# Expert blocks with 64-row remainders, a third weight buffer, and pair weights found by matmul in the route

## The chip, the cores and the metric

The kernel runs on one core of one Trainium2 chip. The metric is device time in microseconds; three runs of the kernel before gave a median of 1706.33 us (1705.12 to 1709.56). All times in the profile are microseconds from the start of its span unless marked ns.

## What is computed

The input x has 4 sequences of 512 tokens with 256 features (2048 tokens, 16 tiles of 128), and a context of 4 x 64 tokens. Four layers follow each other, each with an attention and a feed-forward part. Three of the feed-forward parts are mixtures of experts, and only these are touched:

```
logits = x @ router                      # 8 experts (7 in layer 1)
top2, weights of the two                 # every token has TOP = 2 pairs
for each token t and its experts e:
    y[t] += w[t, e] * (silu(xn[t] @ Wg[e]) * (xn[t] @ Wu[e])) @ Wd[e]
```

Layer 0 (stage `e0`) has 8 experts with a hidden width of 704, layer 3 (`e3`) has 8 with 512, layer 1 (`e1`) has 7 with 256 and a shared expert beside them. Everything is float32. Which expert gets how many of the 4096 pairs is known only at run time.

## The kernel before, in words

The stages run one after the other: attention `a0`, experts `e0`, attention `a1`, layer 1's attention `l1`, experts `e1`, lookup and FP4 feed-forward `f2`, attention `a3`, experts `e3`. `experts` (L1790 on) calls `normalise`, `route` and, for layers 0 and 3, `blocks`; for layer 1 `kept_blocks`, which is not changed.

**route** (L1951 on) ranks the pairs by expert. TensorE counts and ranks them into the bank `small`; VectorE turns the counts into the first block of each expert, each pair's slot, the owner (expert) of each block, and one-hot tables `place_hot` (place in the block) and `at_hot` (which block). Two tables of `numbers` are filled by GpSimd from `at_hot` (L2083), two by VectorE. 32 matmuls (L2035) then find, for each slot, the number of its pair; VectorE makes of it the row of the token, `token`, and `pair`, the address of the pair's weight. ScalarE writes the two weights of every token into `weight_of`, and SyncE copies that table to DRAM (`w_pairs`, L2062) and waits for it, on the same queue on which late weights were sent before. TensorE fills its waits with products that nobody reads (`stay_busy`, L360): 20, 44 and 16 of 512 columns. GpSimd last gathers the rows of the first two blocks (L2095). The stage ends when all engines are through.

Layers 0 and 3 use the simple layout: every expert's pairs are rounded up to whole blocks of 128 rows, and the number of blocks is its worst case,

```
ROUTED = (TOP * B * S + NE * (P - 1)) // P        # 39
```

Layer 1 already uses `Layout(7, 32)`: 28 full blocks, and 6 mixed ones of four quarters with an expert each, which its route lays out by a longer chain of small steps (L2173 to L2204).

**blocks** (L2297 on) works through the 39 blocks in order, in a hardware loop of two blocks. The queues for block n are:

- SyncE: `load_gate_up` (L1868) reads the owner into a register and loads gate and up weights of the expert, two transfers (704 KB each in layer 0, 512 KB in layer 3), into one of two buffers `wgu`, as soon as the up product two blocks earlier is done. The down weights of all experts lie in SBUF.
- GpSimd: gathers the rows of block n (`fetch`, L2353) two blocks ahead, sends the results of block n - 4 by an adding scatter into `y_sum` (`send`, L2367), and gathers the 128 weights of a block (`fetch_weight`, L2359). A send waits until the send before has landed.
- TensorE: gate product of block n, the expert's number into a register, turning the rows of block n + 1, up product of n, down product of n - 1. The gate and up products have 128 x 128 pieces of the weights as the stationary side and 128 turned rows moving, 2 per chunk of 128 hidden columns (L2394); the down product has the hidden rows stationary and 256 columns moving (L2418).
- ScalarE: silu (L2454). VectorE: copies the turned rows (L2466), multiplies gate and up (L2473), and weighs the result while it copies it (L2481); in layer 0 it also quantises a chunk of the FP4 weights every second block (`rounds.round`), 18 in all.

In the end SyncE waits for the sends; in layer 3 it then copies `y_sum` to the output.

## Time and profile before

| | us |
|---|---|
| median of 3 runs | 1706.33 |
| profiled execution, its own time | 1702.23 |
| its span | 1700.0 |
| TensorE matmul busy | 1486.8 (87%) |
| TensorE weight loads busy | 1125.1 (66%) |
| VectorE, ScalarE, GpSimd busy | 941.7, 536.2, 509.6 |
| mean granted TensorE clock | 0.947 |
| stage e0: route from 146.6, blocks from 176.0, tail to about 491 | |
| stage e3: route from 1435.3, blocks from 1462.0, end 1700 | |

PE is TensorE, PEld its weight loads, DVE VectorE, ACT ScalarE, POOL GpSimd, SP SyncE; PEq and SPq are the sequencers of TensorE and SyncE. The profiled execution is one of the kernel's executions, 4.1 us below the median. PEclk is the granted clock of TensorE as a share of 2.4 GHz. A float32 matmul shows as two records. Matmul ends are modelled, so starts are the safer marks.

### The profile page before, as it was taken

To read this page: it belongs to the slowest core of one execution; us is meant where nothing else is said; L and a number is where in the kernel's file an instruction comes from. 1 tells how busy PE (TensorE), PEld (TensorE's weight loads), DVE (VectorE), ACT (ScalarE), POOL (GpSimd) and SP (SyncE) were. 2 spreads that over 40 slices of the span, in tenths; PEclk is the share of its full clock that TensorE was granted. 3 is DMA by queue.
4 is the path that set the end of the run, shared out by engine and by line. 5 is a ranking of instruction groups with operands and counts; after the bars stand their busy time and mean duration, and the time that the engine had idled before them with its cause. 6 is when DMAs were issued, how large, how long until landed. Compare 5 with 4: busy or idle time off the path is not lost. (4 is left out here: it accounts for less than half of the span.)

```text
span 1700.0 us, 33505 instructions
## 1 busy us (share of the span) xinstructions
PE 1486.8 (87%) x11960; PEld 1125.1 (66%) x11961; DVE 941.7 (55%) x2396; ACT 536.2 (32%) x1143; POOL 509.6 (30%) x549
## 2 busy tenths in 40 slices
PE   4887899999979987799987999668888888899995
PEld 3664799999967863355554555346666665699995
DVE  4556244444438977766645633579877566422221
ACT  2331111111137754455542256233322333011010
POOL 0102344444410002111112223345342110466663
PEclk9999999999988998899998999889989999999998
DMA  4109677777720005434304122210000005588885
GB/s 142 49 2 299 215 221 220 221 219 222 218 79 1 2 1 153 131 99 115 90 21 151 64 88 82 68 41 19 1 1 1 1 2 179 180 243 240 233 237 148
DMA packets 127860, 199.85 MB, mean 118 GB/s; under 512 B 20224, under 2 KB 77312, under 8 KB 127552
## 3 DMA queue, kind: packets, MB, share of 16 engines
q1 hardware_dynamic: 107104, 169.15, 30.7%
q0 software_dynamic: 20640, 29.16, 8.3%
q8 instruction: 72, 1.18, 0.3%
q14 instruction: 44, 0.36, 0.1%
HBM read 165.71 MB, written 34.64 MB: 118 GB/s over the span
## 5 line engine op out<-in xcount | busy, mean ns | idle before, releaser
L1576 DVE TENSOR_REDUCE l1a_nm<-l1a_sc 128x1 f32<-128x512 f32 (+3 forms) x256 | 107.1, 482 | 53.7 <-PE l1a_sc L1712 53.7
L2454 ACT ACTIVATE e0b_sg<-e0b_gp 128x640 f32<-128x640 f32 x78 | 33.5, 481 | 266.2 <-PE e0b_gp L2394 266.2
L2367 POOL DMA_INDIRECT y_sum<-e0b_yb,e_token x39 | 63.1, 1619 | 140.6 <-DVE e0b_yb L2481 137.6
L2454 ACT ACTIVATE e3b_sg<-e3b_gp 128x512 f32<-128x512 f32 x39 | 23.3, 597 | 190.0 <-PE e3b_gp L2394 190.0
L2367 POOL DMA_INDIRECT y_sum<-e3b_yb,e_token x39 | 62.7, 1607 | 61.5 <-DVE e3b_yb L2481 58.6
L1710 PE MATMUL l1a_sc<-l_stack_k,l_stack_q 128*128 128x512 bf16 (+3 forms) x256 | 59.1, 309 | 16.7 <-PEq L1354 14.9
L1710 PEld LDWEIGHTS l1a_sc<-l_stack_k,l_stack_q 128*128 128x128 bf16 x256 | 25.3, 99 | 60.8 <-issue 26.8
L2473 DVE TENSOR_TENSOR e0b_hT<-e0b_up,e0b_sg 128x640 f32<-128x640 f32 x39 | 32.1, 824 | 57.8 <-PE e0b_up L2394 57.8
L1471 POOL TENSOR_TENSOR xn<-xn 128x512 f32<-128x512 f32 x8 | 10.1, 1265 | 178.2 <-DVE xn L1439 178.2
L2394 PEld LDWEIGHTS e0b_gp<-e0b_xT,e0k_wgu 128*128 128x128 f32 x480 | 58.4, 197 | 1.9 <-DVE e0b_xT L2466 0.9
L1246 DVE TENSOR_REDUCE a_nm<-a_sc 128x8 f32<-128x512 f32 x64 | 39.7, 683 | 35.8 <-PE a_sc L1096 35.8
L2394 PE MATMUL e0b_gp<-e0b_xT,e0k_wgu 128*128 128x128 f32 x480 | 58.7, 280 | 0.5 <-DVE e0b_xT L2466 0.5
L2473 DVE TENSOR_TENSOR e3b_hT<-e3b_up,e3b_sg 128x512 f32<-128x512 f32 x39 | 27.0, 691 | 57.6 <-PE e3b_up L2394 57.6
L1738 PE MATMUL l1a_st<-l_stack_q,l_stack_k 128*128 128x512 bf16 (+3 forms) x256 | 56.6, 302 | 0.0
L2575 PE MATMUL e1b_gu<-e_kgu,e1b_xT 128*128 x112 | 54.6, 611 | 1.7 <-DVE e1b_xT L2670 1.7
L2394 PEld LDWEIGHTS e0b_gp<-e0b_xT,e0b_wgu 128*128 128x128 f32 x456 | 53.8, 192 | 2.5 <-issue 1.5
L2394 PE MATMUL e0b_gp<-e0b_xT,e0b_wgu 128*128 128x128 f32 x456 | 54.1, 275 | 1.4 <-DVE e0b_hT L2473 1.4
L1190 POOL CAST a_nmp<-a_nm 128x32 bf16<-128x32 f32 x16 | 8.8, 553 | 154.2 <-DVE a_nm L1246 154.2
L3256 PE MATMUL f_yp<-f2w_down,f_hT 128*128 128x256 f32 x192 | 49.6, 413 | 4.6 <-DVE x L3110 4.0
L2541 POOL DMA_INDIRECT e_xb<-x_rows,e_token x32 | 30.2, 945 | 77.8 <-PE e1b_xp L2560 67.3
L2481 DVE TENSOR_SCALAR e0b_yb<-e0b_yp,e0k_weight 128x256 f32<-128x256 f32 x39 | 18.9, 484 | 62.4 <-PE e0b_yp L2418 62.4
L2466 DVE COPY e3b_xT<-e3b_xp 128x256 f32<-128x256 f32 x39 | 16.5, 424 | 58.4 <-PE e3b_xp L2388 58.4
(645 smaller groups left out, 4099.7 us busy)
## 6 DMA issues: line engine op xcount, KB each, us to landing
e3k_wgu<-in_L_ffn_W SPq DMA_DIRECT2D x40, 512.0 KB, 4.9
e3b_wgu<-in_L_ffn_W SPq DMA_DIRECT2D x38, 512.0 KB
e0k_wgu<-in_L_ffn_gate_proj SPq DMA_DIRECT2D x20, 704.0 KB, 4.3
e0k_wgu<-in_L_ffn_up_proj SPq DMA_DIRECT2D x20, 704.0 KB, 5.5
e0b_wgu<-in_L_ffn_gate_proj SPq DMA_DIRECT2D x19, 704.0 KB, 4.3
e0b_wgu<-in_L_ffn_up_proj SPq DMA_DIRECT2D x19, 704.0 KB, 5.6
x_rows<-xn SPq DMA_DIRECT2D x3, 2048.0 KB, 8.4
l_parts<-l1p_split SPq DMA_DIRECT2D x16, 384.0 KB, 3.1
```

Of the source, the lines that this page charges most:

```text
L1246: nc.vector.tensor_reduce(nm[:, :, r, :], bank[r][:].rearrange("p t (h l) -> p t h l", l=L), AX_X, ALU.max, negate=True).then_inc(max_done, 1)
L1576: nc.vector.tensor_reduce(nm[:, g % 2, q, i:i + 1], sc[q], AX_X, ALU.max, negate=True).then_inc(max_done, 1)
L1710: nc.tensor.matmul(sc[q], of_head(1, n)[:, q * P:(q + 1) * P], of_head(0, n)[:, 0:(q + 1) * P], start=True, stop=False)
L1738: nc.tensor.matmul(to(k), of_head(0, n)[:, k * P:(k + 1) * P], of_head(1, n)[:, k * P:], start=False, stop=False)
L2367: pool.indirect_dma_start(y_sum, bass.IndirectOffsetOnAxis(ap=token[:, n:n + 1], axis=0), yb[n % 2][:], None, compute_op=ALU.add).then_inc ...
L2394: last = nc.tensor.matmul(dst[:, f, :], wgu[j][:, k, at + f * P:at + (f + 1) * P], xT[j][:, k, :], start=(k == 0), stop=(k == KC - 1))
L2454: last = nc.scalar.activation(sg[rows, chunks, :], gp[rows, chunks, :], ACT.Silu)
L2473: last = nc.vector.tensor_tensor(hT[j][rows, chunks, :], from_up, sg[rows, chunks, :], ALU.mult)
L2481: nc.vector.tensor_scalar(yb[j][:], yp[:], plan.weight[:, bass.ds(n, 1)], None, ALU.mult).then_inc(y_copied, 1)
L2541: pool.indirect_dma_start(xb[n % 2][:], None, x_rows, bass.IndirectOffsetOnAxis(ap=token[:, order[n]:order[n] + 1], axis=0))\
L2575: last = nc.tensor.matmul(gu[n % 2][:], xT[n % 2][:, k, :], wgu[:, bass.ds(e, 1), k, :].rearrange("p a f -> p (a f)"), start=(k == 0), sto ...
L3256: last = nc.tensor.matmul(yp[:], hT[:, f, :], dT[:, f, :], start=(f == 0), stop=(f == FC - 1))
```

## The change

- The layout of layers 0 and 3 becomes `HALVES = Layout(8, 64)`: 32 full blocks and 4 mixed ones of two halves of 64 rows, each with an expert of its own, 36 blocks and 40 units of weights. The mixed blocks stand at positions 4, 13, 22 and 31 of the order. Layer 1 keeps its layout; its tables lose 5 columns.
- Three buffers `wgu` instead of two; a load waits for the up product of the block that used the buffer last.
- In a mixed block the turned rows are the stationary side, 64 columns per half, and up to 512 columns of the half's own weights move; the hidden rows are then turned by TensorE (`turn_hidden`), copied by ScalarE, and the down product takes its second half's weights from `mixed_d`, which ScalarE has copied beforehand.
- A mixed block is sent twice, each time with the other half's rows directed to spare rows.
- The weight of each slot's pair is split into three bf16 parts, multiplied into `at_hot` (three products on GpSimd, three on VectorE), found by 32 more matmuls in the route and summed by VectorE. The DRAM table, its write and the 39 gathers per layer are gone. The last `stay_busy` of the route has 10 products instead of 16.
- The loops over blocks are written out instead of run in hardware loops, and TensorE reads the expert's number right ahead of the down product.

```diff
-ROUTED = (TOP * B * S + NE * (P - 1)) // P
+HALVES = Layout(NE, P // 2)
 QUARTERS = Layout(NE - 1, P // 4)
+ROUTED = HALVES.blocks
...
@@ SummedBlocks
-            self.weight_of = ...; self.pair = ...
+            self.HELD = 3
+            self.send = st.enter_context(nc.sbuf_tensor(f"{tag}k_send", [P, HALVES.owners], U32))
@@ route, TensorE, behind the matmuls that find the tokens
                     if plan is not None:
-                        stay_busy(idle[:], 16)
+                        pe.wait_ge(weighted, 3 * TOP)
+                        for t in range(T):
+                            for k in range(TOP):
+                                last = nc.tensor.matmul(found_weight, place_hot[k][:, t, :], weight_hot[k][:, t, :, :],
+                                                        start=(t + k == 0), stop=(t == T - 1 and k == TOP - 1))
+                        last.then_inc(weight_made, 1)
+                        stay_busy(idle[:], 10)
@@ route, SyncE
-                        sp.wait_ge(tabled, 1)
-                        sp.wait_ge(weighed, 3)
-                        sp.dma_start(w_pairs.rearrange("(p n) a -> p (n a)", p=P), plan.weight_of[:]).then_inc(tabled, 16)
-                        sp.wait_ge(tabled, 17)
@@ route, GpSimd
+                        (weight_part[0..2]: five operations of 32 columns, once the weights are there)
                     pool.wait_ge(step, 30)
                     (numbers[0], numbers[1])
+                    if plan is not None:
+                        pool.wait_ge(parted, 5)
+                        for i in range(3):
+                            nc.gpsimd.tensor_tensor(weight_hot[1][:, :, i, :], at_hot[1][:], bcast(weight_part[i][:, :, 1], 2, NB), ALU.mult)\
+                                .then_inc(weighted, 1)
                     (gathers of the first two blocks' rows)
@@ route, VectorE: layout of all layers by full and odd parts (the old simple branch goes), and before the token
+                        for i in range(3):
+                            nc.vector.tensor_tensor(weight_hot[0][:, :, i, :], at_hot[0][:], bcast(weight_part[i][:, :, 0], 2, NB), ALU.mult)\
+                                .then_inc(weighted, 1)
...
+                        dve.wait_ge(weight_made, 1)
+                        nc.vector.tensor_reduce(plan.weight[:, 0:NB], found_weight.rearrange("p i b -> p b i"), AX_X, ALU.add)
@@ blocks, SyncE
+                    for k in range(1, len(block_of)):
+                        if k >= plan.HELD:
+                            sp.wait_ge(up_made, block_of[k - plan.HELD] + 1)
+                        plan.load_gate_up(sp, owner, owner_of[k], k % plan.HELD)
@@ blocks, GpSimd
-                    def fetch_weight(n): ...
                     def send(n):
                         pool.wait_ge(y_copied, n + 1)
+                        for i, (block_n, at, done, value) in enumerate(sent):
+                            if block_n == n:
+                                if i:
+                                    pool.wait_ge(*sent[i - 1][2:])
+                                pool.indirect_dma_start(y_sum, bass.IndirectOffsetOnAxis(ap=plan.send[:, at:at + 1], axis=0), yb[n % 2][:],
+                                                        None, compute_op=ALU.add).then_inc(done, 16)
@@ blocks, TensorE
+                        if is_mixed(n):
+                            for lo in range(0, chunks * P, BANK):
+                                hi = min(lo + BANK, chunks * P)
+                                for k in range(KC):
+                                    for u, unit in enumerate(units_of[n]):
+                                        rows = slice(u * HALF, (u + 1) * HALF)
+                                        last = nc.tensor.matmul(flat(dst)[rows, lo:hi], xT[n % 2][:, k, rows],
+                                                                wgu[unit % plan.HELD][:, k, at + lo:at + hi], start=(k == 0), stop=(k == KC - 1))
...
+                    for n in range(NB):
+                        gate(n)
+                        if n + 1 < NB:
+                            turn_rows(n + 1)
+                        if n and is_mixed(n - 1):
+                            turn_hidden(n - 1)
+                        up_product(n)
+                        ... down(n - 1)
@@ blocks, VectorE
+                        if rounds is not None and n % 2:
+                            rounds.round(dve, n // 2)
+                    weigh_out(NB - 1)
```

## Rows read from the trace of the kernel before

**Rows 1.** Windows of the block stages: span, busy by engine (count), granted clock, DMA share, GB/s.

```profile
176.00:187.40 11.40, 9.46 (x52) 7.89 (x53) 2.27 (x6) 2.14 (x3) 3.77 (x4) 0.71 0.46 151
187.40:484.00 296.60, 295.93 (x2214) 283.55 (x2214) 131.81 (x331) 32.61 (x76) 133.36 (x110) 1.00 0.71 212
1469.00:1683.00 214.00, 212.35 (x1602) 202.33 (x1602) 60.83 (x114) 22.69 (x38) 130.78 (x110) 1.00 0.78 226
```

**Rows 2.** Timeline of TensorE, a block of layer 0: start us, us, instructions.

```profile
434.57 2.84 PE L2394 MATMUL e0b_gp<-e0b_xT,e0b_wgu 128*128 128x128 f32 x24
...
439.70 1.03 PE L2418 MATMUL e0b_yp<-inner,e0b_hT 128*128 x4
...
442.29 2.84 PE L2394 MATMUL e0b_gp<-e0b_xT,e0k_wgu 128*128 128x128 f32 x24
```

**Rows 3.** Chain that ended last: a block of layer 3, and the tail.

```profile
1657.64 1.78 PE e3b_gp L2394 x16
1659.42 0.22 PE e3b_xp L2388 x2
1659.64 1.79 PE e3b_up L2394 x16
1661.43 1.73 PE e3b_yp L2418 x8
...
1679.53 0.49 DVE e3b_yb L2481
...
1680.87 3.68 DMA y_sum<-e3b_yb,e_token
...
1685.10 1.79 POOLq L2326
```

**Rows 4.** Timeline of TensorE in layer 1: a full block's gate and up, a mixed block's.

```profile
977.10 1.88 PE L2575 MATMUL e1b_gu<-e_kgu,e1b_xT 128*128 x4
...
980.22 1.92 PE L2572 MATMUL e1b_gu<-e1b_mixed_gu,e1b_xT 128*32 128x512 f32 x16
```

**Rows 5.** DMA issues: KB each, median us to landing.

```profile
e3k_wgu<-in_L_ffn_W SPq DMA_DIRECT2D x40, 512.0 KB, 4.9
e3k_xb<-x_rows,e_token POOLq DMA_INDIRECT x39, 4.7
```

**Rows 6.** Timeline of VectorE in the routes of layer 1 and layer 3.

```profile
935.63 0.16 DVE L2173 TENSOR_SCALAR e1r_held_i<-e1r_small 128x8 uint32<-128x8 f32 x1
...
938.99 0.85 DVE L2214 TENSOR_TENSOR e1r_past<-consts,e1r_begins 128x676 f32<-128x676 f32 x1
...
1441.36 0.17 DVE L2156 COPY e3r_cnt<-e3r_small 128x8 f32<-128x8 f32 x1 [1.11 <-PE e3r_small L2022]
...
1443.54 0.44 DVE L2211 TENSOR_TENSOR e3r_past<-consts,e3r_first 128x273 f32<-128x273 f32 x1
```

**Rows 7.** Line 2083, GpSimd: duration ns min/median/max, first and last start.

```profile
L2083 POOL TENSOR_TENSOR e0r_numbers<-e0r_at_hot,consts x2: 3150/3216/3281, 158.7 to 161.8; 128x624 bf16<-128x624 f32 x2
L2083 POOL TENSOR_TENSOR e1r_numbers<-e1r_at_hot,consts x2: 1235/2258/3282, 943.8 to 944.9; 128x624 bf16<-128x624 f32 x2
L2083 POOL TENSOR_TENSOR e3r_numbers<-e3r_at_hot,consts x2: 3221/3252/3283, 1447.3 to 1450.4; 128x624 bf16<-128x624 f32 x2
```

**Rows 8.** Timeline of TensorE: end of layer 3's route and start of its blocks.

```profile
1455.70 5.30 PE L360 MATMUL e3r_idle<-ones_h,ident_h 128*128 128x512 bf16 x16
...
1462.07 1.02 PE L360 MATMUL e3b_gp<-ones_h,ident_h 128*128 128x512 bf16 x4 [1.07 <-PEq L2005]
```

**Rows 9.** Timeline: end of layer 0's route and start of its blocks.

```profile
166.33 3.32 SPq L2062 DMA_DIRECT2D w_pairs<-e0k_weight_of  x1
...
176.05 1.86 PE L360 MATMUL e0b_gp<-ones_h,ident_h 128*128 128x512 bf16 x4 [3.98 <-PEq L2005]
```

**Rows 10.** DMA queue of instructions in layer 0's and in layer 1's blocks: packets, MB, share.

```profile
q8 instruction: 3, 0.05, 0.1%
...
q8 instruction: 5, 0.08, 0.3%
```

More of the change, by code:

```diff
@@ L195, in build @@
     rows_out = [pool_sem(f"rows_out{j}") for j in range(2)]
-    weight_in = [pool_sem(f"weight_in{j}") for j in range(2)]
     rows_summed = [pool_sem(f"rows_summed{j}") for j in range(2)]
@@ L2416, in down, with turn_hidden @@
+                    def turn_hidden(n):
                         pe.wait_ge(h_done, n + 1)
                         for f in range(FC):
-                            last = nc.tensor.matmul(yp[:], hT[j][:, f, :],
+                            width = min(P, F - f * P)
+                            last = nc.tensor.transpose(hp[0:width, f, :], h[:, f * P:f * P + width], ident)
+                        last.then_inc(h_turned, 1)
+                    def down(n):
+                        if n:
+                            pe.wait_ge(y_copied, n)
+                        own = lay.owner_at(order[n])
+                        e = pe.value_load(owner[0:1, own[0]:own[0] + 1], min_val=0, max_val=plan.E - 1)
+                        first = slice(0, P // len(own))
+                        if is_mixed(n):
+                            pe.wait_ge(mixed_ready, (mixed_at.index(n) + 1) * FC)
+                            pe.wait_ge(h_copied, mixed_at.index(n) + 1)
+                        else:
+                            pe.wait_ge(h_done, n + 1)
+                        for f in range(FC):
+                            last = nc.tensor.matmul(yp[first, :], hT[n % 2][:, f, first],
@@ L2445, in _ @@
-                    down(NB - 1, 0, expert(NB - 1))
+                    stay_busy(flat(gp)[:, 0:S], 4)
+                    turn_rows(0)
+                    for n in range(NB):
+                        gate(n)
[4 more added lines that the diff above has]
+                        up_product(n)
+                        if n == 0:
+                            if LEFT:
+                                pe.wait_ge(padded, 2)
+                            pe.wait_ge(plan.kept, plan.all_kept)
+                        else:
+                            down(n - 1)
```

444 lines of the change are left out of this document (209 added, 235 removed).

## The prediction

> **What bounds the kernel now.** I read the windows by stage first, because only the two stages that the change rebuilds matter: the expert blocks of layer 0 and of layer 3. In both, TensorE works 295.9 of 296.6 us and 212.4 of 214.0 us at a granted clock of 1.00, VectorE is busy less than half, and the DMA engines 0.71 and 0.78 [rows 1]. So these stages last as long as TensorE's instructions, and taking a block out takes its whole TensorE time out. The timeline then gives a block of layer 0: from one gate product to the next 442.29 - 434.57 = 7.72 us, of which the down product is 2.59 [rows 2]. The chain that ended last gives a block of layer 3 with no gap in it: gate 1.78, turning the rows 0.22, up 1.79, down 1.73, together 5.52 us; and it shows the tail, where two sends into y_sum stand in a row, each waiting for the one before to land [rows 3].
>
> **Blocks.** The old bound on blocks is 39, all of 128 rows; the new layout has 32 full and 4 mixed, 36. That removes 3 blocks per layer: 3 x 7.72 + 3 x 5.52 = 39.7 us off, all on the path.
>
> A mixed block multiplies the turned rows (64 wide, two units) as the stationary side with up to 512 weight columns moving, instead of 128 x 128 pieces. The rows for that are the mixed blocks of layer 1: four units side by side make 16 matmul records in 1.92 us, where a full block makes 4 records over the same columns in 1.88 [rows 4]. So outputs on separate partitions run beside each other, and what counts is the moving columns, which are the same 768 + 640 (layer 0) or 512 + 512 (layer 3) as in a full block. I take gate, up and down as unchanged, with the 0.04 us of rows 4 once. What a mixed block adds on TensorE is turning the hidden rows: 6 or 4 transposes at 0.22 / 2 = 0.11 us [rows 3], with the 0.04 some 0.7 and 0.5 us. Four each: 4.8 us. ScalarE's copy out of PSUM and its copies of the second expert's down weights lie beside the up product; VectorE does the same elements. If units did not share TensorE at all, see the first rival. The Trainium skill, "TensorE: Matmul & The Clock Gate", section "Measured speedup vs the span model", gives 2.38 times for three column tiles, not three times. By that rule, applied to two halves (an estimate: 1.6 instead of 2), the sum would be about 13 us more, 1692; the trace's four tiles disagree, since 1.92 against 1.88 is nearly full overlap.
>
> The register load of the expert's number moves on TensorE's queue from behind the gate product to behind the up product. It stands behind 1.79 us of queued matmuls instead of 1.78 [rows 3], so I cost it at nothing; without that cover every block would pay it.
>
> **Loads.** There are 40 unit loads instead of 39, over 36 blocks. A load is issued when an up product ends and lands 4.9 us after its issue in layer 3 [rows 5]; it is needed one block and one down product later, 5.52 + 1.73 = 7.25 us. The third buffer keeps this slack where two units fall into one block, so nothing waits, though DMA work per microsecond grows by 40/36 = 1.11, towards a share of 0.78 x 1.11 = 0.87 at most, less the gathers of weights that go. The row gathers (4.7 us to landing, [rows 5]) now stand on POOL's queue behind a send that may wait for another send, but two blocks ahead of use.
>
> **Route.** Its steps are serial on VectorE. (a) Layout by full and odd parts: in layer 1, which already does this, count to ownership takes 938.99 - 935.63 = 3.36 us, in layer 3 now 1443.54 - 1441.36 = 2.18: +1.18. (b) The ownership test and its sum grow from 273 to 600 elements: 0.44 now, 0.85 for 676, so about 0.76: twice +0.32. (c) Wrapping the owner, two more small steps, +0.2. Sum +2.0 us [rows 6].
> (d) POOL. The two products that fill `numbers` took 3.2 us each for 624 elements beside a busy VectorE, but 1.24 once when layer 1's VectorE was not in its long products [rows 7]. The change adds three more of that kind on POOL (576 elements), and TensorE's new weight products wait for them. Per product 1.14 (free) to 3.0 us (contended). In layer 3: start 1447.3 + 2.0, two numbers 6.0, then the three, of which the first is contended and the others mostly free, 5.6 (bounds 3.4 and 9.0): 1460.9. POOL's own first two row gathers queue behind this, where they used to start from the token alone.
> (e) TensorE: 32 products of 108 columns, then 10 idle-time products. The 16 of before took 5.30 us, a mix of both clocks [rows 8]; from 0.21 to 0.43 per 512 columns the 32 cost 1.4 to 2.9 and the ten 2.1 to 4.3. I take 2.4 + 3.0, since TensorE stands still before found and again before weights. End 1466.3, plus the 1.07 of changing blocks [rows 8]: 1467.3 against 1462.07 now. **+5.2 us** (bounds +1 and +10). What goes, VectorE's shorter token chain and the table write, ended earlier here and gives nothing.
> In layer 0 the same steps start at 158.7 and end at 158.7 + 2.0 + 6.0 + 5.6 + 2.4 + 3.0 + 1.07 = 178.8. There the old end is later, 176.05, with TensorE still for 3.98 us before: the table write of w_pairs is issued at 166.33, behind the late weights on the same queue [rows 9]. That wait goes; +2.7 us remain. But the stillness also cost clock: the first 11.4 us of blocks had a granted clock of 0.71 [rows 1], 3.3 us of lost time. With idle-time products up to 1 us before, as in layer 3, I take 3.0 of it back: **-0.3 us** (bounds -4 and +8).
> Layer 1 changes only by fewer columns beside a busy TensorE: 0.
>
> **Sends.** Removed: 39 weight gathers per layer, which lie on POOL and DMA, off the path: 0. Added: a second send per mixed block, chained. From rows 3 a chained send takes 4.5 (copy 1680.02 to landing 1684.55) to 5.1 us (to the next issue, 1685.10), say 4.8. In layer 0 the delay 2 x 4.8 - 7.72 = 1.9 is gone one block later. In layer 3 it is 2 x 4.8 - 5.52 = 4.1, recovered by 0.7 per block. The last mixed block is number 31 of 0 to 35, so 4.1 - 2 x 0.7 = **+2.7 us** reach the tail (1.4 to 3.8).
>
> **Sum.** -39.7 + 4.8 + 5.2 - 0.3 + 2.7 = -27.3 us on the profiled execution's 1702.2 (span 1700.0 and 2.2 around it): 1674.9. The median of the runs shown is 4.1 higher, so 1679.
>
> **Rivals.**
> *A, the halves take turns (0.05).* A pair of 64-wide products would run one after the other. Place: the mixed blocks. Price: gate, up and down a second time, 4 x 7.5 + 4 x 5.3 = 51 us: 1679 + 51 = 1730, slower than before. It decides from the point where 27 of the 51, a little over half of the second unit's time, is exposed. Against it: [rows 4], though those are 32 wide.
> *A2, they share only in part (0.03).* The same place with a quarter of the second unit's time exposed: 51 / 4 = 13 us, 1692. For and against as A. The skill's 2.38 for three tiles would lie near this.
> *B, code loading (0.04).* The loops become straight code. Now 3 fetches fall into 297 us of layer 0's blocks; layer 1's unrolled blocks make 5 in 110 us with light DMA [rows 10]. Unrolled, layer 0 and 3 would need about 30, beside DMA engines at 0.8. A fetch with no lead at all would cost up to a row gather's 4.7 us [rows 5]; at 2 us each it is 60 us: 1739. For it only that no row has both conditions; against it that layer 1's blocks have no such gap. The Trainium skill, "Runtime: NRT & Kernel Launch", section "Instruction fetch mechanics", says sequential code is fetched ahead and taken branches are what stall; by that this rival falls.
> *C, a queue runs late at mixed blocks (0.15).* The load slack in layer 3, 7.25 - 4.9 less the time to issue two transfers, is under 2.4 us, and the row gather behind two chained sends has 2 x 5.52 us less the sends' 9.6. If each of the 8 mixed blocks costs 1 to 2 us of waiting: 1687 to 1695.
> *D, the route at its upper bounds (0.1):* +5 and +8 more: 1692. At its lower bounds (0.06): 1671.
> Forecast as summed: 0.57.
>
> **Numbers.** Predicted 1679. The range runs from both routes at their low bounds to C or D: 1669 to 1693, leaving A, B and joint mishaps out. 0.3% is 5 us, about what a measurement of this kernel can tell. Faster by more: 0.91 (forecast, A2, C, D). Within it: 0.02, a half-exposed A or B. Slower: 0.07 (rest of A and B).
>
> **What would show it.** 36 gate groups per layer; full blocks at 7.72 and 5.52 us; mixed ones at 8.4 and 6.0, the pair's records ending together. Records in turn would show A, TensorE idle with no releaser B, TensorE waiting for a wgu or xb transfer after blocks 4, 13, 22, 31 C. In the routes, POOL's five products ahead of the gathers, block stage starts near 179 and 5 us later than now. Weight matmuls that don't wait for POOL would prove (d) wrong, and a tail of the old length the sends' term.

## The result, and the profile after

| us | before | after |
|---|---|---|
| median (range) of 5 runs each | 1706.33 (1702.2 to 1709.6) | 1719.04 (1715.3 to 1724.1) |
| profiled execution, its span | 1702.23, 1700.0 | 1723.26, 1721.4 |
| mean granted TensorE clock | 0.947 | 0.934 |

The ratio of the times is 1.0092, 95% interval [1.0073, 1.0112]: the change makes the kernel slower by 0.9%, where 1679 us, 1.6% faster, was predicted. The two profiled executions lie 21 us apart, because one is at the low end of its runs and the other near the high end; the stages below are compared within one execution each.

Windows of the block stages after, same columns as [rows 1]: the start of layer 0's blocks, then both stages, then 9 us around one break.

```profile
182.20:190.80 8.60, 6.64 (x53) 5.84 (x53) 2.27 (x6) 3.17 (x6) 1.89 (x2) 1.00 0.78 292
190.80:480.00 289.20, 281.34 (x2054) 252.19 (x2055) 121.91 (x314) 39.56 (x95) 93.76 (x71) 0.98 0.71 220
1481.50:1697.00 215.50, 204.03 (x1452) 179.08 (x1452) 55.24 (x104) 27.80 (x53) 90.58 (x69) 0.97 0.78 228
399.00:402.00 3.00, 2.44 (x12) 2.44 (x13) 2.79 (x10) 0.00 (x0) 2.20 (x2) 0.50 0.15 11
402.00:405.00 3.00, 3.00 (x14) 2.91 (x14) 1.33 (x4) 0.00 (x0) 1.56 (x2) 0.50 0.37 76
405.00:408.00 3.00, 3.00 (x17) 2.65 (x17) 1.13 (x3) 0.00 (x0) 1.66 (x2) 0.94 0.54 102
```

TensorE is no longer busy throughout: 7.9 us are missing in layer 0 and 11.5 in layer 3 (0.7 and 1.6 in [rows 1]), though 3 blocks are gone from each. Around each break the granted clock is 0.50, for 3.4 us at the first and the third and for 6.8 us at the second and the fourth. The breaks, in TensorE's timeline:

```profile
322.81 0.44 PE L2387 MATMUL e0b_xp<-consts,e0k_xb 128*128 128x128 f32 x2 [2.61 <-DMA e0k_xb<-x_rows,e_token]
...
399.56 0.69 PE L2387 MATMUL e0b_xp<-consts,e0k_xb 128*128 128x128 f32 x2 [3.94 <-DMA e0k_xb<-x_rows,e_token]
...
1578.50 0.44 PE L2387 MATMUL e3b_xp<-consts,e3k_xb 128*128 128x128 f32 x2 [3.23 <-DMA e3k_xb<-x_rows,e_token]
...
1636.45 0.69 PE L2387 MATMUL e3b_xp<-consts,e3k_xb 128*128 128x128 f32 x2 [4.68 <-DMA e3k_xb<-x_rows,e_token]
```

Each time a row gather is late. From gate product to gate product these blocks take 12.18, 14.63, 10.62 and 12.56 us in place of 7.72 and 5.52, so with the slow clock behind them the four breaks cost 4.5 + 6.9 + 5.1 + 7.0 = 23.5 us. What was late stands in GpSimd's waits (us in total, times, longest), where the kernel before waited for `y_sum` once in each layer:

```profile
POOL y_sum L2371 <- DMA y_sum<-e0b_yb,e0k_send: 110.2, 24, 6.6
...
POOL y_sum L2371 <- DMA y_sum<-e3b_yb,e3k_send: 56.6, 21, 4.7
```

GpSimd's timeline from the first mixed block of layer 0 on shows how it comes about:

```profile
231.73 1.59 POOL L2371 DMA_INDIRECT y_sum<-e0b_yb,e0k_send  x1 [5.18 <-DVE e0b_yb L2527]
237.72 1.57 POOL L2371 DMA_INDIRECT y_sum<-e0b_yb,e0k_send  x1 [4.40 <-DMA y_sum<-e0b_yb,e0k_send]
239.59 1.01 POOL L2360 DMA_INDIRECT e0k_xb<-x_rows,e_token  x1 [0.30 <-issue]
244.61 1.58 POOL L2371 DMA_INDIRECT y_sum<-e0b_yb,e0k_send  x1 [4.00 <-DMA y_sum<-e0b_yb,e0k_send]
246.49 1.02 POOL L2360 DMA_INDIRECT e0k_xb<-x_rows,e_token  x1 [0.30 <-issue]
253.01 1.58 POOL L2371 DMA_INDIRECT y_sum<-e0b_yb,e0k_send  x1 [5.50 <-DMA y_sum<-e0b_yb,e0k_send]
```

The second send (237.72) goes out when the first has landed, and the sends that follow it wait for the one before: the queue runs at the pace of its own landings, 6.0, 6.9, 8.4 us, and a row gather stands behind each send. SyncE's timeline has the loads beside them:

```profile
237.00 0.38 SPq L1872 DMA_DIRECT2D e0b_wgu<-in_L_ffn_gate_proj  x1
...
244.71 0.38 SPq L1872 DMA_DIRECT2D e0b_wgu<-in_L_ffn_gate_proj  x1
```

In the kernel before, a send went out 2.7 us after a load (435.64 after 432.97) and landed 4.3 us after its issue (median), 7.0 after the load's. Now it goes out together with the load (237.72 and 237.00) and the next one can go only 6.9 us later, at 244.61, again together with a load (244.71). The delay keeps itself up, one send per load, and each mixed block adds one link.

The DMA packets tell what is late, the rows themselves or only the report of their landing. In the profile's DMA view, packets of GpSimd's transfers are `software_dynamic`, those of SyncE's loads `hardware_dynamic`. After the issue at 237.72, first up to 242.0 and then from 242.0 to 243.5 (packets, MB, share):

```profile
q1 hardware_dynamic: 460, 1.25, 90.6%
...
q0 software_dynamic: 178, 0.25, 76.2%
q1 hardware_dynamic: 84, 0.19, 32.6%
```

The 128 rows of the send are among the 178: the first moves 4.5 us after the issue (242.24), beside the last packets of the load, and the last has moved by 243.50, 1.1 us before the next send goes out (244.61). So it is the rows that are late. Over all sends of layer 0's blocks the median time from the issue to the first row's packet is 2.4 us in the kernel before and 4.5 us in the changed one.

Layer 3 is less regular: there the steps between sends behind the first mixed block run from 4.5 to 7.6 us, and the seven from 1512.66 to 1550.36 are 5.4 us in the mean, where a block takes 5.52. At the end the late sends hang behind the last product. The chain that ended last, to be read against the tail in [rows 3]:

```profile
1698.13 3.78 DMA y_sum<-e3b_yb,e3k_send
...
1702.64 3.85 DMA y_sum<-e3b_yb,e3k_send
```

The copy to the output goes out at 1711.05, 23.1 us after the last gate product's start (1687.97); before it was 15.1.

### The profile page after: what moved, and what is told of

Its sections match the earlier page's. It is cut to its first block and busy times, and to the rows that moved or that the text cites. A ratio compares the mean times of both kernels' runs of the same rounds, so it can differ in the third digit from the quotient of the medians.

```text
span 1721.4 us, 31704 instructions
## 1 busy us (share of the span) xinstructions
PE 1467.2 (85%) x11688; PEld 1079.2 (63%) x11720; DVE 942.6 (55%) x2399; ACT 550.3 (32%) x1182; POOL 439.3 (26%) x483
## 5 line engine op out<-in xcount | busy, mean ns | idle before, releaser
L2371 POOL DMA_INDIRECT y_sum<-e0b_yb,e0k_send x40 | 63.0, 1574 | 180.8 <-DMA y_sum<-e0b_yb,e0k_send 110.2
L2480 ACT ACTIVATE e0b_sg<-e0b_gp 128x640 f32<-128x640 f32 x64 | 27.5, 482 | 221.6 <-PE e0b_gp L2402 221.6
L2371 POOL DMA_INDIRECT y_sum<-e3b_yb,e3k_send x40 | 62.9, 1572 | 120.1 <-DVE e3b_yb L2527 63.5
L1713 PE MATMUL l1a_sc<-causal_h,ident_h 128*128 128x128 bf16 x256 | 46.7, 222 | 20.7 <-PEq L1355 16.2
L2520 DVE TENSOR_TENSOR e0b_hT<-e0b_up,e0b_sg 128x640 f32<-128x640 f32 x32 | 26.4, 825 | 55.5 <-PE e0b_up L2402 53.8
L1739 PE MATMUL l1a_st<-l_stack_q,l_stack_k 128*128 128x512 bf16 (+2 forms) x254 | 56.1, 301 | 0.0
L2527 DVE TENSOR_SCALAR e3b_yb<-e3b_yp,e3k_weight 128x256 f32<-128x256 f32 x36 | 17.4, 484 | 65.1 <-DMA y_sum<-e3b_yb,e3k_send 37.2
L1711 PE MATMUL l1a_sc<-l_stack_k,l_stack_q 128*128 128x256 bf16 (+3 forms) x226 | 50.0, 295 | 2.1 <-DVE l1a_nm L1577 1.8
L2402 PE MATMUL e0b_up<-e0b_xT,e0b_wgu 128*128 128x128 f32 x400 | 51.6, 288 | 0.0
L2402 PEld LDWEIGHTS e0b_up<-e0b_xT,e0b_wgu 128*128 128x128 f32 x400 | 49.9, 205 | 0.0
```

Of the source, the lines that this page charges most:

```text
L1711: nc.tensor.matmul(sc[q], of_head(1, n)[:, q * P:(q + 1) * P], of_head(0, n)[:, 0:(q + 1) * P], start=True, stop=False)
L1713: last = nc.tensor.matmul(sc[q][:, q * P:(q + 1) * P], ident_h[:], causal_h[:], start=False, stop=True)
L1739: nc.tensor.matmul(to(k), of_head(0, n)[:, k * P:(k + 1) * P], of_head(1, n)[:, k * P:], start=False, stop=False)
L2371: pool.indirect_dma_start(y_sum, bass.IndirectOffsetOnAxis(ap=plan.send[:, at:at + 1], axis=0), yb[n % 2][:], None, compute_op=ALU.add).th ...
L2402: last = nc.tensor.matmul(dst[:, f, :], wgu[units_of[n][0] % plan.HELD][:, k, at + f * P:at + (f + 1) * P], xT[n % 2][:, k, :], start=(k = ...
L2480: last = nc.scalar.activation(sg[rows, chunks, :], gp[rows, chunks, :], ACT.Silu)
```

## Experiments

Times are medians, "ratio" is to the kernel before in runs on the same chip, with its 95% interval. Each diff is against the changed kernel unless it says otherwise.

**No mixed blocks.** `HALVES = Layout(NE, P)`: 39 whole blocks, the rest of the change kept.

> The changed kernel with no mixed block: both experts layers again run 39 blocks of 128 rows of one expert each (7.72 and 5.52 us), one send per block; three weight buffers, the blocks written out one by one and the weights found by TensorE stay. Chain theory (the second send of a mixed block puts the queue of sends one load behind, and each send then waits for the one before): with one send per block POOL waits for y_sum under 10 us in all, sends land in 3.6 to 5.0 us, no gap of TensorE for xb inside the blocks; only the longer routes (+3.5 and +5.9) and the first gate product on a faster clock (-2.8) are left: 1706 + 5 to 8, so 1710 to 1715 us. Three-buffers theory (loads bunched by the third buffer delay the row gathers): the breaks of 2.6 to 4.7 us stay, and with two more blocks each the time is 1735 or more. Code loading: gaps on several engines at once stand in the blocks, 1725 or more.

1716.73 us, ratio 1.0074 [1.0049, 1.0099]. GpSimd waits for `y_sum` not at all in e0 and 9.2 us in e3, sends land in 4.4 and 4.3 us, no break, full blocks 7.72 and 5.52. So neither the third buffer nor the straight code breaks anything. Without a single mixed block the change still costs 11 to 13 us, where at most 9 were expected; the run with the route alone, below, comes back to this.

**One send per mixed block.** The second half is not sent; its rows are missing from the result.

```diff
-                for at in lay.owner_at(order[n]):
+                for at in lay.owner_at(order[n])[:1]:
```

> The changed kernel, with the send of the second half of every mixed block left out (so these rows of the result are missing); products, loads and gathers as they are. Chain theory: POOL waits for y_sum under 10 us in each layer, landing back at 3.6 to 5.0 us, the four breaks (4.5, 6.9, 5.1 and 7.0 us) are gone and the tails shorter by 1 to 3 us each: 1719 - 23.5 - 4 = 1691 us (1688 to 1696). Three-buffers theory: sends have little to do with it, the row gathers are late as before, 1712 or more.

1690.04 us, 0.9904 [0.9873, 0.9936]: the eight sends left out are worth 29 us. No break. In e0 the waits for `y_sum` are gone; in e3 the expectation of under 10 us was wrong, they are still there, only never long enough to stop TensorE:

```profile
POOL y_sum L2371 <- DMA y_sum<-e3b_yb,e3k_send: 49.3, 15, 5.8
```

**No loads.** Gate and up weights are loaded for three units only.

```diff
-                    for k in range(1, len(block_of)):
+                    for k in range(1, plan.HELD):
...
-                            pe.wait_ge(gu_in[unit % plan.HELD], 32 * (unit // plan.HELD + 1))
+                            pe.wait_ge(gu_in[unit % plan.HELD], 32)
```

> The changed kernel with the weights of gate and up loaded for the first three units only (later blocks multiply by stale ones, the result is wrong in value but the work of the engines is the same); both sends of a mixed block stay. Theory that a send beside a weight load lands when the load ends: without loads a send lands in 4.3 us or less throughout, the second sends are caught up within one block, no breaks: 1719 - 23.5 - 4, near 1691 us, perhaps less by the waits for a load. Theory that the added send is slow of itself, or that POOL's own issue work takes the time: the landing stays at 6 to 8 us and the breaks stay, 1710 or more.

1684.85 us, 0.9876 [0.9849, 0.9903], with both sends of every mixed block. The landing of a send, in the answer for its tile (min/median/max), of e0:

```profile
DMA to landing us min/median/max: 3.7/3.8/4.3
```

From issue to the first row's packet it is now 2.1 us in the median, with the work of VectorE and GpSimd the same. GpSimd still waits for `y_sum`, 17.7 us in e0 and 42.4 in e3, but never over 3.2 us: in e3 the steps behind a second send are 4.6 us of a block of 5.52, so the queue catches up by 1 us per block, and there is no break. So the second send alone stops nothing; it takes loads beside it.

**Half the rows in the first send**: partitions 0 to 63.

```diff
-pool.indirect_dma_start(y_sum, bass.IndirectOffsetOnAxis(ap=plan.send[:, at:at + 1], axis=0), yb[n % 2][:],
+rows = slice(0, lay.unit if at >= lay.full and (at - lay.full) % lay.per == 0 else P)
+pool.indirect_dma_start(y_sum, bass.IndirectOffsetOnAxis(ap=plan.send[rows, at:at + 1], axis=0), yb[n % 2][rows, :],
```

> The changed kernel, where the first send of a mixed block covers partitions 0 to 63 alone (its own rows; the other 64 went to spare rows and added nothing that is kept), so 64 rows less in each mixed block. Theory that a send's landing is set by the end of the load beside it: half the rows change nothing, 1719 within 4 us, breaks stay. Theory that a send costs by its rows: the first send of a mixed block lands in about 2.2 to 3.3 us in place of 6.5, the queue is caught up, breaks mostly gone, 1697 or less.

1719.46 us, 1.0067 [1.0045, 1.0088], with four breaks at the same blocks: the number of rows is not the price.

**Another chain for the second sends.** They add into a table `y_side`, which the result leaves out, and wait only for each other.

```diff
+                        if n in side:
+                            if side[n]:
+                                pool.wait_ge(side_summed, 16 * side[n])
+                            pool.indirect_dma_start(y_side, bass.IndirectOffsetOnAxis(ap=plan.send[:, at:at + 1], axis=0), yb[n % 2][:],
+                                                    None, compute_op=ALU.add).then_inc(side_summed, 16)
```

> The changed kernel, where the second send of each mixed block adds into a second table in DRAM and waits only for the one before it of its own kind (8 of 80 sends); the result leaves this table out. Every send, load, gather and product is still made; only the chain is shorter, one link per block. Theory that the link the second send adds to the chain is what brings the breaks: POOL waits for y_sum as in the kernel with one send (few us in e0), breaks gone, 1692 us (1687 to 1697). Theory that the bytes or POOL's issue time of the second sends bring them (chain or not): breaks stay, 1712 or more.

1694.13 us, 0.9947 [0.9930, 0.9964]. All products, loads, gathers and sends are made, and the breaks are gone, though GpSimd still waits 53.9 us for `y_sum` in e3: it is the link in the chain that costs, 25 us of it, not the bytes and not GpSimd's issuing.

**Three row buffers**, gathers a block earlier.

```diff
-                        pool.wait_ge(x_turned, n - 1)
-                        pool.indirect_dma_start(xb[n % 2][:], None, x_rows,
+                        if n > 2:
+                            pool.wait_ge(x_turned, n - 2)
+                        pool.indirect_dma_start(xb[n % 3][:], None, x_rows,
```

> The changed kernel with three row buffers in place of two, each row gather one block earlier, and the sends in the same places of time. Theory of the chained sends (their delay of one load each is what counts): TensorE no longer waits for xb, but the queue is as late as before, and the weighing of block n waits for the send of block n - 2, so the same delay comes out there: gaps put down to yb in place of xb, 1719 within 5 us. Theory that POOL's order (the gather stands behind a waiting send) is the cause: the breaks are gone and nothing takes their place, 1695 or less.

1717.82 us, 1.0082 [1.0050, 1.0113]. TensorE's timeline has the breaks under another name:

```profile
402.45 0.91 PE L2447 MATMUL e0b_yp<-inner,e0b_hT 128*128 x3 [2.27 <-DVE e0b_yb L2536]
...
1641.05 1.22 PE L2447 MATMUL e3b_yp<-inner,e3b_hT 128*128 x2 [7.06 <-DVE e3b_yb L2536]
```

VectorE can't refill `yb` before the send two blocks back has landed. The row gather behind the waiting send is where the lateness comes out first, not its cause.

**Split loads.** The half for up goes out about 4 us after the half for gate (`between` is `(gate_made, block_of[k - plan.HELD] + 2)`).

```diff
             for at, m in ((0, self.w_gate), (self.F, self.w_up)):
+                if at and between is not None:
+                    sp.wait_ge(*between)
```

> The changed kernel, where of each unit's load only the half for gate goes out when the up product ends; the half for up waits for the gate product of the next block but one to be made (about 4 us later). All sends stay. Theory that a send lands with the load it runs beside: a send issued together with the first half now lands with that half, after some 4 us, so the queue gains 2 to 3 us per block on the blocks and is caught up before the next mixed block; POOL waits for y_sum 30 us or less in e0 (110 before), the four breaks are gone: 1719 - 23.5 - 4, so 1691 us (1687 to 1697). Theory that the DMA engines simply have too much to carry: the bytes are the same, the landing stays at 6 us or more and the breaks stay, 1712 or more.

1718.8 us, 1.0098 [1.0068, 1.0128]: the time missed, though half of the reason held. In e0 GpSimd catches up (44.1 us of waiting for 110.2) and neither break is left, which makes e0's blocks 8 us shorter than in the changed kernel. e3's got 7 us longer, with both breaks still there and late up weights at three of the four mixed blocks (1.1 to 1.6 us):

```profile
POOL y_sum L2374 <- DMA y_sum<-e3b_yb,e3k_send: 97.7, 32, 5.1
```

In the changed kernel's tail two sends with nothing beside them stand 4.5 us apart (1698.13 and 1702.64); a block takes 5.52 us in e3 and 7.72 in e0. So e3 has at best 1 us per block to catch up with, and with split loads one load or the other runs beside most sends. That this is why e3 got worse was not shown by a run.

**A cheaper route.** One of VectorE's three weight products ahead of the token chain, two behind; 70 and 6 filler products of TensorE in place of 44 and 10.

```diff
-                        stay_busy(idle[:], 44)
+                        stay_busy(idle[:], 70)
...
-                        for i in range(3):
+                        for i in range(1):
                             nc.vector.tensor_tensor(weight_hot[0][:, :, i, :], at_hot[0][:], ...
...
                         nc.vector.tensor_copy(token[:, 0:NB], row_f[:]).then_inc(routed, 1)
+                        for i in range(1, 3):
+                            nc.vector.tensor_tensor(weight_hot[0][:, :, i, :], at_hot[0][:], ...
```

> The changed kernel with another order in the route: VectorE makes one of its three weight products ahead of the token chain and two behind it, TensorE's filler before the found product goes from 44 to 70 matmuls (its idle 6.5 us shrinks to under 1) and the one behind the weights product from 10 to 6. If the weight products ahead of the token chain and the cold clock of the two products are what made the route longer: the found product 2.10 to about 1.1 us, the weights product 3.06 to about 1.6, the token chain some 2.5 us earlier, each of the two stages of blocks starts 2 us earlier: 1719 - 4 = 1715 (1713 to 1717). If the route waits for another thing (the row gather's landing is bound by its issue, or POOL's products), no change: 1719 within 1.5. The breaks in the blocks stay in both.

1717.37 us, 1.0080 [1.0058, 1.0102]. The found product took 1.21 us (2.10 before), but from the start of the route to e0's gate product of block 1 it is 40.4 us in place of 41.4 (148.0 to 188.40, 149.4 to 190.80), 1 us gained where 2 were expected; the weights product did not get shorter (3.06), since TensorE again stood still for 3.16 us before it. In e3 the gain went into waiting 2.5 us for the second load. The total can't be told from the changed kernel's.

**All three together:** the diffs of split loads, three row buffers and the cheaper route.

> Split loads, three row buffers and the reordered route together, result as the reference's. By the theory of chained sends beside loads: 1719 - 28 (breaks and tails) - 4 (route) = 1687 us (1683 to 1693), that is 1% faster than the kernel before. By the rival theories of the single runs 1705 or more.

1718.85 us, 1.0094 [1.0069, 1.0119]. A miss for the same reason: e0 without a break, e3 with five gaps for `yb` of up to 4.1 us.

**Mixed blocks in e0 alone**, split loads there, the cheaper route, and 39 whole blocks in e3 (`WHOLE` is `Layout(NE, P)`).

```diff
-        lay = QUARTERS if shared else HALVES
+        lay = QUARTERS if shared else HALVES if F % P else WHOLE
```

> e0 with mixed blocks and split loads, e3 with 39 whole blocks and loads as in the changed kernel, both with the reordered route; result as the reference's. From the run without mixed blocks (1716.7): e0's blocks 3 less (-23.2), its four mixed blocks +6 and waits for loads +1.5, the route -2.4 and -1: 1697.6 (1693 to 1702), no break in either layer. If split loads do not keep e0's queue up, or e3's short blocks break without mixed blocks too, 1705 or more.

1703.9 us, 0.9994 [0.9985, 1.0003]: the best with a whole result, and level with the kernel before. No break in either layer; windows of the two block stages:

```profile
188.00:470.00 282.00, 277.47 (x2057) 248.88 (x2056) 123.25 (x317) 39.46 (x95) 93.84 (x71) 1.00 0.79 228
1479.00:1690.00 211.00, 202.66 (x1531) 194.12 (x1529) 58.85 (x110) 21.49 (x36) 93.40 (x72) 1.00 0.77 216
```

**Both layers mixed, e3 with a side table, result whole.** `y_side` starts with zeros, SyncE copies it to the output after its last send, GpSimd adds `y_sum` onto it (first run); or both are read into SBUF, added by VectorE and written (second run).

```diff
+                        sp.wait_ge(side_summed, 16 * len(side))
+                        for g in range(PARTS):
+                            sp.dma_start(part(rows, g), part(y_side, g)).then_inc(written, 16)
...
+                            pool.dma_start(part(rows, g), part(y_sum, g), accum_op=ALU.add, max_dma_last_dim=4096)
```

and in the second run, on VectorE:

```diff
+                            dve.wait_ge(main_in[g], 16)
+                            nc.vector.tensor_tensor(held(xn, g), held(xn, g), held(x, g), ALU.add).then_inc(both_added, 1)
```

> Mixed blocks in both layers, result as the reference's: e0 with split loads and one chain; e3 with its second halves added into a table of their own (zeros at first), which SyncE copies to the output after the last of them, and GpSimd adds the table of the others onto it at the end; reordered route in both. Theory of the chain's length: e3's blocks run without a break, found product to last product 216 to 218 us (230 with 39 whole blocks): 1704 - 13.6, and the end costs 3 to 8 us more for the adding copy: 1695 (1691 to 1699), faster than both. If the early copy of 2 MB or the zeros disturb the queue of sends, or the adding copy takes 15 us or more: 1703 or more.

> As the run with e3's second halves in a table of their own, but the two tables are added in SBUF: SyncE loads the side table while the last blocks run and the main one at the end in four parts, VectorE adds each part and SyncE writes it out. The adding copy took 19 us from its issue to the end of the span, the plain copy of the kernel before 11. Four loads landing after some 6 us, four additions of 1.1 us beside them and four stores of 6 us overlap: about 14 us, 5 less than the adding copy: 1707 - 5 = 1702 (1697 to 1706). If loads and stores do not overlap, 18 us and no gain, 1707.

1706.97 us, 1.0015 [0.9994, 1.0036], and 1706.27, 1.0010 [0.9989, 1.0030]. In both, e3's blocks run without a break (start of the found product to start of the last down product 217.4 and 215.0 us, 230.0 with whole blocks). The adding copy goes out at 1678.11 of a span of 1697.4, 19.3 us, where the plain copy takes 10.9 (1689.1 to 1700.0); the way through SBUF takes 15.5 (1678.45 to 1694.0). Their runs scatter more than any other's here (1699 to 1720, 1696 to 1713), and why is open, and the profiled executions are the fastest of each. The expected 1695 and 1702 were both missed, the first by the adding copy's 19.3 us. On the median neither beats the kernel before.

**Where the other 11 us are: loops, route, queue.** Three runs with 39 whole blocks each. First SyncE's and ScalarE's parts in hardware loops again; then all of the old `blocks` (loops, two buffers) with the new route alone; then that with the 78 weight gathers put back on GpSimd's queue, into a tile nobody reads.

```diff
+                    with sp.Fori(0, (NB - plan.HELD) // plan.HELD) as i:
+                    with act.Fori(1, NB) as n:
...
-            self.HELD = 3
+            self.HELD = 2
...
+                        pool.indirect_dma_start(plan.unused[:, n:n + 1], None, w_pairs,
+                                                bass.IndirectOffsetOnAxis(ap=token[:, n:n + 1], axis=0)).then_inc(weight_in[n % 2], 16)
```

> The changed kernel without mixed blocks, its SyncE and ScalarE parts of the blocks in hardware loops as in the kernel before, TensorE, VectorE and GpSimd written out. At the end of e0's blocks the changed kernels stand still for about 4 us between the last send's landing and the next stage's first load, the kernel before for under 1. Theory that the long written-out program of the engine which waits last (SyncE) makes that: the standstill falls to 1 us, the time from 1716.7 to about 1713.5. Theory that it lies with the other engines' programs or with the semaphores added: no change, 1716.7 within 1.5.

> One part of the change alone: the weights found by TensorE in the route, no table and no weight gathers; the blocks are those of the kernel before, 39 whole ones in hardware loops with two weight buffers. By the stage times of the changed kernel: e0's route +3.5, e3's +5.9 us, so 1704 + 9 = 1713 (1710 to 1716). Theory that the written-out programs of TensorE and VectorE make the standstill of 3 to 4 us at the end of e0's blocks: it is gone here, the next stage's first load 4.4 us after the last send's issue as in the kernel before (7.9 in the changed one). Theory that the added semaphores or the other engines make it: it stays, and the time is 1716.

> The run with the route alone, and the 78 weight gathers of the kernel before put back on GpSimd's queue, into a tile that nothing reads (the weights still come from the route; one small table is written for them in each route). Theory that the standstill at the end of e0's blocks came with taking the weight gathers off GpSimd's queue: it goes back from 8.1 to 4.4 us after the last send's issue, and the time from 1717 to 1713 or less, though it does more work. Theory that the standstill comes with the new route (its semaphores, its longer GpSimd part): it stays at 8 us and the time is 1717 or a little more.

1718.91 us, 1.0101 [1.0073, 1.0128]; 1717.5, 1.0059 [1.0038, 1.0081]; 1720.2, 1.0085 [1.0062, 1.0109]. The route alone makes the kernel slower by 10 us, and the intervals of these runs and of the one without mixed blocks overlap, so straight code and the third buffer cost too little to be told. The stages account for it: of the changed kernel's differences listed below, those that do not come from mixed blocks are 3.5 + 5.9 (routes) - 2.8 (clock) + 3.5 + 1.7 (two standstills) = 11.8 us. It also shows, as all kernels without the gathers do, the standstill at the end of e0's blocks, and the gathers take it away. GpSimd's last send in e0 and its next work, with the route alone:

```profile
490.82 1.55 POOL L2345 DMA_INDIRECT y_sum<-e0b_yb,e_token  x1 [2.92 <-DMA y_sum<-e0b_yb,e_token]
499.89 0.31 POOL L635 MEMSET a_bias<- 128x256 bf16 x1 [7.51 <-issue]
```

and with the gathers back:

```profile
492.65 1.57 POOL L2357 DMA_INDIRECT y_sum<-e0b_yb,e_token  x1 [2.83 <-DMA y_sum<-e0b_yb,e_token]
498.45 0.41 POOL L638 MEMSET a_bias<- 128x256 bf16 x1 [4.24 <-issue]
```

The trace's records of the sequencers say where it stands still: GpSimd's closing drain, which begins with the last send's issue, takes 4.4 us in the kernel before, 7.9 in the changed one, 8.0 with the route alone and 4.5 with the gathers back, while SyncE had seen the last landing about 4 us after the issue in each. The total of that run did not fall as expected. It also writes a table in each route, and 2.1 us went at the start of e0's blocks: the first two take 16.7 us in place of 14.6, with the clock at 0.79 from 190 to 196. The rest was not followed.

**Two gathers near the end of e0** added to the kernel with mixed blocks in e0 alone.

```diff
                         send(n)
+                        if LEFT and n + 2 < NB:
+                            pool.indirect_dma_start(again[:], None, x_rows,
+                                                    bass.IndirectOffsetOnAxis(ap=token[:, order[n]:order[n] + 1], axis=0)).then_inc(once_more, 16)
```

> The kernel with mixed blocks and split loads in e0 alone (1703.9 us), and two row gathers into a tile that nothing reads, behind the third and the second of e0's last four sends, where the kernel before had its last two weight gathers. Theory that the standstill at the end of e0's blocks depends on a gather on GpSimd's queue near the end (within three sends of it): 4.5 us after the last send's issue in place of 7.9, so 1703.9 - 3.4 = 1700.5 (1698 to 1702), 0.2% faster than the kernel before. Theory that it takes the weight gathers all along the blocks, or another thing of that run: no change, 1704.

1703.87 us, 0.9998 [0.9979, 1.0017]; the standstill stays, 8.1 us from the last send to the next load (475.40 to 483.46). A gather near the end is not what removes it. Whether it takes them all along, or the table write of that run, is open.

## Why the prediction was wrong

**The step that failed is the sends' term**: a chained send at "say 4.8", a delay that in layer 0 "is gone one block later" and in layer 3 is "recovered by 0.7 per block", +2.7 in all. The step was wrong beside loads, and with it the recovery. The 4.8 were read from two sends at the very end [rows 3], where no load runs, and for that they are right: with the loads left out the steps behind a second send are 4.0 and 4.5 us in layer 0 and 4.6 in layer 3, and the queue does catch up. Beside a load the steps in layer 0 are 6 to 8.9 us up to the first break, and then there is nothing to recover with: 6.9 + 8.4 for two blocks of 7.72. In layer 3 they are 5.4 in the mean for blocks of 5.52. The term was 2.7 and measured 23.5 (breaks) + 8.0 (tail) = 31.5 us in the profiled execution; taking the link out gave back 25 (side table) to 29 us (one send). DMA shares of 0.7 to 0.8 were in front of the prediction [rows 1] and were used for the loads only, not for the sends that go through the same engines.

The Trainium skill bears on this, in "DMA: Bandwidth & Descriptors", section "Queues, rings and completion order": a DMA's semaphore increment is a write that lands only after every earlier write of the same DMA engine, across its queues. By that a send could be reported late though its rows had long been written. The trace does not need that: the rows themselves set off late, 4.5 us after the issue beside a load, 2.1 with no loads, and most of the delay is there. Whether the rule adds to it, no run here shows. Nor do the runs tell by what order the DMA engines let the load's packets go first.

**Rival C** named the place (the row gather behind two chained sends), with 1 to 2 us for each of 8 mixed blocks. It was taken as a wait that ends with its block. It does not end, it adds up until the slack of two row buffers is used, which came after the second and after the third mixed block of each layer, and then the clock is at 0.50 for 3.4 or 6.8 us. Its slack, "2 x 5.52 us less the sends' 9.6", used the same 4.8.

The other terms, e0 then e3:

- *Blocks removed:* -23.2 and -16.6, as predicted; full blocks are 7.72 and 5.52.
- *Mixed blocks*, predicted 0.7 and 0.5 each, measured 1.5 and 1.3: the one itself 8.10 and 5.93, the next 8.62 and 6.20, 0.1 on each block beside them. TensorE's timeline at the next one: turning the hidden rows 0.66 as predicted, but the down product in pairs 2.74 for 2.59, and at each change of shape about 0.1. The halves do run side by side, which refutes rivals A and A2, and disagrees with the 2.38 (for three tiles) of the Trainium skill ("TensorE: Matmul & The Clock Gate", section "Measured speedup vs the span model"): the first two products of a pair start together, and gate takes 2.73 us to the next kind of work, 2.68 in a full block.

```profile
225.12 0.82 PE L2423 MATMUL e0b_hp<-consts,first_weights 128*128 128x128 f32 x6
...
285.10 0.64 PE L2397 MATMUL e0b_gp<-e0b_wgu,e0b_xT 128*64 128x512 f32 x1
285.10 0.64 PE L2397 MATMUL e0b_gp<-e0k_wgu,e0b_xT 128*64 128x512 f32 x1
```

- *Route:* +3.5 and +5.9, predicted +2.7 and +5.2. The contention between GpSimd and VectorE was the right mechanism, and both sides paid. What was left out is VectorE's own weight products, ahead of the token chain: the found product (TensorE) is done at 174.5, and VectorE turns to it at 176.23. And 1.1 us of e0's 3.5 come before any of this: the 20 filler products at its start take 5.95 us to the count in place of 4.88, at a granted clock of 0.72 in place of 1.00, after the longer standstill named below.

```profile
170.71 4.32 POOL L2099 TENSOR_TENSOR e0r_weight_hot<-e0r_at_hot,e0r_weight_part 128x576 bf16<-128x576 f32 x3
...
172.31 4.00 DVE L2254 TENSOR_TENSOR e0r_weight_hot<-e0r_at_hot,e0r_weight_part 128x576 bf16<-128x576 f32 x3
176.23 0.18 DVE L2265 COPY e0r_token_p<-e0r_small 128x36 f32<-128x36 f32 x1
```

- *Clock at the start of e0's blocks:* -2.8, predicted -3.0. The stretch of 11.4 us at 0.71 [rows 1] is 8.5 us at 1.00.
- *Weight gathers removed*, costed at nothing: +3.5 us at the end of e0, unforeseen. Last send to the next stage's first load: 4.4 us (486.40 to 490.79) before, 7.9 (483.62 to 491.52) after.
- *Ahead of e0's route*, in no term either: TensorE stands still for 4.0 us between the last product of `normalise` and the route's first, where it was 2.3, while SyncE is still issuing loads of the FP4 weights. All runs with the new route have it (3.9 to 4.4 us in all but one, 2.9 in that), also those with the old `blocks`. The cause was not followed.
- *Rival B:* refuted, no gap without a releaser in the blocks, though 17 instruction fetches fall into 289 us of layer 0's, and the run with the old loops is no faster. What was cited there from the Trainium skill ("Runtime: NRT & Kernel Launch", section "Instruction fetch mechanics"), that sequential code is fetched ahead, agrees with this.

The sum: e0 -23.2 + 6.0 + 3.5 - 2.8 + 11.4 + 3.5 = -1.6, from route start to next stage -2.0 (344.2 to 342.2). e3 -16.6 + 5.2 + 5.9 + 12.1 + 8.0 = +14.6, from route start to the copy of the result +14.9 (253.8 to 268.7). Together 12.9, against 12.7 between the medians; that they agree so well is luck, since the 1.7 us ahead of e0's route are not in the 12.9, and single executions of the changed kernel lie from 1715 to 1724. What is left of the 21 us between the profiled executions lies, but for these 1.7, in stages that the change doesn't touch.

## What to carry to other kernels

Count a chain of dependent transfers by the step that it has beside the traffic of its stage, never by one read from a quiet tail, and compare it with the period of the loop: above or near the period, an added link is not a delay but a debt that stays, and it comes out in whatever the same queue carries next. Another buffer only moves where it comes out; a shorter chain removes it. Before a part is moved to the engines of a serial stage, price the work of every engine that stands ahead of the next step, here VectorE's as well as GpSimd's.

## What the runs showed of the hardware that was not expected

- A small transfer sets off late behind a large one on another queue: from the issue of an adding scatter to its first row's packet the median is 2.1 us without loads and 4.5 us in the changed kernel's layer 0, where loads of 1.4 MB go out with it.
- An adding scatter of 128 rows of 1 KB lands in 3.8 us without loads, 4.3 when it goes out 2.7 us behind a load of 1.4 MB, and when it goes out with one, the send that waits for it can go only 6.9 us later; with 64 rows in the first send the breaks were the same.
- Without the weight gathers on GpSimd's queue the end of e0's blocks took 3.5 us longer, and it is GpSimd's closing drain that takes them (7.9 us for 4.4); with them back it was 4.5 us again. No cause was found.
- An adding DMA copy of 2 MB from DRAM to DRAM, issued by GpSimd, took 19.3 us where the plain one, issued by SyncE, took 10.9.
- Two bf16-writing products at once, one on GpSimd and one on VectorE, slow each other: VectorE took 2.74 us for two of 576 columns in layer 0's route, 0.90 for two of 544 in layer 1's, where GpSimd had finished its own.
